# A graph network in one core: h and the attended rows turned by DMA instead of TensorE, biases side by side, a new order of work

## Time and profile before

| | |
|---|---|
| three runs | 2445.72, 2445.99, 2448.67 us; median 2445.99 |
| profiled execution | 2447.97 us, its span 2445.9 us |
| TensorE busy | 2336.1 us (96%), granted clock 0.98 in the mean |
| VectorE, ScalarE, GpSimd busy | 1980.6 (81%), 1848.4 (76%), 1636.8 us (67%) |
| DMA | 164.96 MB in 480426 packets |

### The profile page before, as it was taken

The page is one execution under the profiler, slowest core; times in us unless marked ns, Lnnn a source line. Parts: engine busy times, 40 slices in busy tenths (PEclk is TensorE's granted clock), DMA queues, the critical chain, the costliest instruction groups (busy, mean ns, idle before and its releaser), DMA issues.

```text
span 2445.9 us, 79908 instructions
## 1 busy us (share of the span) xinstructions
PE 2336.1 (96%) x26448; PEld 1722.6 (70%) x26448; DVE 1980.6 (81%) x8952; ACT 1848.4 (76%) x4660; POOL 1636.8 (67%) x2194
## 2 busy tenths in 40 slices
PE   4599999999999999999999999999999999999985
PEld 3367777777777777777777777777777777777753
DVE  7668888888888888888888888888888888888863
ACT  4467788777778877878777787877777777777763
POOL 1147677767767776777777677777767777776762
PEclk8799999999999999999999999999999999999997
DMA  6113333333323333333333333233333323333321
GB/s 201 55 37 64 60 69 65 72 66 66 68 60 67 67 70 68 67 68 60 67 68 67 70 65 70 60 67 68 67 69 65 70 60 67 67 68 69 60 50 36
DMA packets 480426, 164.96 MB, mean 67 GB/s; under 512 B 414224, under 2 KB 480016, under 8 KB 480016
## 3 DMA queue, kind: packets, MB, share of 16 engines
q1 hardware_dynamic: 479008, 159.86, 31.9%
q10 hardware_dynamic: 1008, 0.00, 0.0%
HBM read 46.53 MB, written 12.58 MB: 24 GB/s over the span
## 4 chain that ended last, share of the span: by engine, by line
PE 83%; POOL 4%; issue 3%; DMA 2%; DVE 2%; ACT 0%; SPq 0%; DVEq 0%; POOLq 0%; ACTq 0%
PE bank L146 21%; PE bank L148 21%; PE bank L147 21%; PE bank L1536 4%; PE bank L1474 4%; PE bank L1523 2%; DMA pT<-p 2%; PE bank L1430 2%; PE bank L1490 1%; PE bank L1492 1%; PE bank L1491 1%; PE bank L1581 1%; PE bank L1579 1%; PE bank L1578 1%; POOL p L629 1%
## 5 line engine op out<-in xcount | busy, mean ns | idle before, releaser
L146 PE MATMUL bank<-w_hi,dir_hT_hi 128*128 128x384 f16 x1728 | 564.5, 327 | 0.0
L148 PE MATMUL bank<-w_hi,dir_hT_lo 128*128 128x384 f16 x1728 | 564.5, 327 | 0.0
L147 PE MATMUL bank<-w_lo,dir_hT_hi 128*128 128x384 f16 x1728 | 564.4, 327 | 0.0
L765 ACT ACTIVATE probs<-minus_scores,minus_max 128x128 f32<-128x128 f32 x1536 | 488.2, 395 | 75.6 <-DVE minus_max L1017 75.6
L629 POOL TENSOR_TENSOR p<-probs,p 128x512 f16<-128x512 f32 x384 | 447.5, 1166 | 124.0 <-ACT p L772 124.0
L146 PE MATMUL bank<-hT_hi,w_hi 128*128 128x128 f16 x2304 | 400.4, 220 | 6.5 <-DVE w_lo L301 3.3
L147 PE MATMUL bank<-hT_lo,w_hi 128*128 128x128 f16 x2304 | 400.4, 220 | 0.0
L148 PE MATMUL bank<-hT_hi,w_lo 128*128 128x128 f16 x2304 | 400.3, 220 | 0.0
L1017 DVE CUSTOM_DVE_ANT_0 minus_scores<-bank,minus_score_bias 128x128 f32<-128x128 f32 x1536 | 343.2, 285 | 16.1 <-issue 13.5
L637 POOL TENSOR_TENSOR raw_weights<-raw_weights,gain_offset 128x384 f32<-128x384 f32 x192 | 192.4, 1002 | 151.5 <-ACT raw_weights L852 151.5
L147 PEld LDWEIGHTS bank<-w_lo,dir_hT_hi 128*128 128x128 f16 x1728 | 169.5, 98 | 112.7 <-issue 1.3
(11 more groups left out here) (177 smaller groups left out, 7259.4 us busy)
## 6 DMA issues: line engine op xcount, KB each, us to landing
x<-in_x SPq DMA_DIRECT2D x64, 192.0 KB, 2.5
dir_adj_tile<-in_adj SPq DMA_DIRECT2D x192, 64.0 KB, 2.1
out<-raw_weights SPq DMA_DIRECT2D x64, 192.0 KB, 2.1
adj_tile<-in_adj SPq DMA_DIRECT2D x128, 64.0 KB, 2.1
pT<-p SPq DMA_TRANSPOSE x384, 3.1
raw_weights<-in_L_gnn_Wq SPq DMA_DIRECT2D x2, 576.0 KB, 4.8
raw_weights<-in_L_gnn_Wk SPq DMA_DIRECT2D x2, 576.0 KB, 5.9
raw_weights<-in_L_gnn_Wv SPq DMA_DIRECT2D x2, 576.0 KB, 7.6
```

The lines of the kernel that those rows point to most:

```text
L146: pe.matmul(out, stat[0], move[0], start=first, stop=False)
L147: pe.matmul(out, stat[0], move[1], start=False, stop=False)
L148: return pe.matmul(out, stat[1], move[0], start=False, stop=last)
L765: last = act.activation(probs[:, i, :], scores[:, i, :], ACT.Exp, bias=nmax[:, t.slot(), i:i + 1], scale=-1.0)
```

## The change

1. h is split before it is turned: ScalarE makes the high half of h from SBUF (`att_hi`, `dir_hi`), GpSimd (`att_lo`) or VectorE (`dir_lo`) the low half, both f16, side by side (`h16`, `dh16`); one DMA transpose on SP's queue (`turn_h`, `dir_turn_h`) turns both halves at once. The attended rows of `last` likewise: scaled in place in PSUM, split (`attended_hi`, `attended_lo`), turned (`turn_o`). All f32 transposes of TensorE in the rounds but `turn_e` go.
2. `bias_rows` also holds the own bias in rows 64 and 96. The right bias is added with rows 0 to 63 and the own bias with rows 64 to 127, one right after the other (`right_self_biases`); the left bias uses rows 0 to 63.
3. A new list of steps for every engine. `project_left` of `lower` and the steps that follow on its similarity move from the end of a round to the start of the next, `project_v` of `last` one round earlier, `project_self` behind `project_right`, the write of the result two rounds later (`LAST_ROUND` is 5 instead of 3 behind). `h16`, `dh16` and x's load get more lead. The small loads of ACT's queue move to SP's.

```diff
-OPENED, LAST_ROUND = 1, G - 1 + 3
+OPENED, LAST_ROUND = 1, G - 1 + 5
...
-                low = bias_rows[32:33, first:first + 3]
...
+                for row, of in ((32, slice(0, 3)), (96, slice(1, 2))):
+                    low = bias_rows[row:row + 1, first + of.start:first + of.stop]
+                    dve.scalar_tensor_tensor(out=low, in0=self.raw_bias[row:row + 1, of],
...
+                def turn_h(t):
+                    if t is None:
+                        return
+                    wait_apart(sp, (hT_ready, t.count(-1, 16)), (h_lo, t.count()), (v_psum, t.count(-2)))
+                    sp.dma_start_transpose(hT[:, t.slot(), :, :],
+                                           h16[t.slot()][:, :, :].rearrange("p a n -> p (a n)")).then_inc(hT_ready, 16)
+
+                def turn_o(t):
...
+                def dir_turn_h(t):
+                    if t is None:
+                        return
+                    wait_apart(sp, (d["hT_ready"], t.count(-1, 16)), (d["h_lo"], t.count()), (d["u_psum"], t.count(-2)),
+                               (d["r_psum"], t.count(-2)), (d["s_psum"], t.count(-2)))
+                    sp.dma_start_transpose(dhT[:, t.slot(), :, :],
+                                           dh16[t.slot()].rearrange("p a n -> p (a n)")).then_inc(d["hT_ready"], 16)
...
                 def step(n_):
+                    att_load_adj(n_.first(-2))
+                    write(n_.last(5))
                     dir_load_adj(n_.single(0))
+                    turn_probs(n_.last(3), 0)
+                    dir_turn_h(n_.single(0))
                     turn_probs(n_.last(3), 2)
-                    load_x(n_.first(-2))
-                    turn_probs(n_.last(3), 0)
+                    turn_probs(n_.last(3), 1)
+                    turn_h(n_.last(2))
+                    dir_turn_h(n_.upper(1))
                     dir_load_adj(n_.upper(1))
-                    turn_probs(n_.last(3), 1)
+                    turn_o(n_.last(3))
                     turn_probs(n_.first(-1), 0)
-                    att_load_adj(n_.first(-2))
                     turn_probs(n_.first(-1), 1)
                     turn_probs(n_.first(-1), 2)
                     dir_load_adj(n_.lower(0))
                     att_load_adj(n_.last(1))
-                    write(n_.last(3))
+                    dir_turn_h(n_.lower(0))
+                    turn_h(n_.first(-2))
+                    load_x(n_.first(-3))
...
+                def att_lo(t):
+                    if t is None:
+                        return
+                    wait(pool, h_hi, t.count())
+                    pool.tensor_tensor(h16[t.slot()][:, 1, :], h[:, :], h16[t.slot()][:, 0, :], ALU.subtract).then_inc(h_lo, 1)
...
+                def dir_hi(t):
...
+                    act.activation(dh16[t.slot()][:, 0, :], dh[:, :], ACT.Copy).then_inc(d["h_hi"], 1)
...
+                def dir_lo(t):
+                    if t is None:
+                        return
+                    wait(dve, d["h_hi"], t.count())
+                    dve.tensor_tensor(dh16[t.slot()][:, 1, :], dh[:, :], dh16[t.slot()][:, 0, :], ALU.subtract).then_inc(d["h_lo"], 1)
...
+                def bias_of(t, part, bank, rows):
+                    pe.matmul(bank[:, 0:D], each_32nd[rows, :], bias_rows[rows, ROW[t.kind] + part, :], start=True, stop=False)
+
                 def project(t, part, bank, ready):
-                    weights, w = WEIGHTS[t.kind], part
-                    pe.matmul(bank[:, 0:D], first_and_33rd[:, :], bias_rows[:, ROW[t.kind] + part, :], start=True, stop=False)
...
+                def right_self_biases(t):
+                    if t is None:
+                        return
+                    wait(pe, d["l_lo"], t.count())
+                    wait(pe, d["ctx_ready"], t.count(-1))
+                    bias_of(t, 2, r_bank, slice(0, 64))
+                    bias_of(t, 1, own_bank, slice(64, 128))
```

More of the change, by code:

```diff
@@ L223, in __init__ @@
                 self.count["turned"] += len(self.work) if transposed else 0
-                self.count["bias"] += keeps if transposed and groups[0][1] else 0
+                self.count["bias"] += 1 if groups[0][1] else 0
                 self.count["kept"] += keeps
@@ L516, in _ @@
                 W2_upper.load_vectors(sp)
+                turn_h(first[1])
+                load_x(first[2])
+                att_load_adj(first[2])
                 dir_load_adj(single[0])
-                load_x(first[2])
+                dir_turn_h(single[0])
                 W2.ready(sp)
@@ L526, in _ @@
                 dir_load_adj(lower[0])
+                dir_turn_h(lower[0])
+                turn_h(first[2])
+                load_x(first[3])
                 run_rounds(step)
@@ new lines, in step @@
+                    left_hi(n_.lower(1))
+                    dir_input(n_.single(0))
+                    dir_hi(n_.single(0))
+                    norm_context(n_.upper(2))
+                    sides_hi(n_.lower(1))
+                    exponents(n_.last(3), 2)
+                    right_hi(n_.lower(1))
+                    v_hi_split(n_.last(3))
+                    weighted_own(n_.lower(1))
+                    probs_hi(n_.last(3), 1)
+                    probs_hi(n_.last(3), 2)
+                    q_evict(n_.first(-1))
@@ L1242, in step @@
                     scaled_denominator(n_.lower(1))
+                    v_lo_split(n_.last(3))
+                    scaled_eps(n_.lower(1))
+                    drop_masked(n_.first(-2))
+                    add_to_x(n_.upper(2))
+                    att_stats(n_.last(2))
+                    att_mean_var(n_.last(2))
+                    att_stats(n_.first(-2))
+                    att_var_eps(n_.last(2))
+                    row_max(n_.single(0))
                     context(n_.lower(1))
-                    scaled_eps(n_.lower(1))
@@ L1284, in step @@
+                    dir_lo(n_.lower(0))
                     denominator(n_.upper(1))
[L1285 to L1293 removed]
@@ L1619, in step @@
                     combine(n_.upper(1))
+                    project_v(n_.last(2))
                     similarity(n_.lower(0))
-                    project_left(n_.lower(0))
-                    att_turn_h(n_.first(-2))
-                    project_self(n_.lower(0))
                 def turn_v_bias(pe):
@@ L1687, in _ @@
                 similarity(lower[0])
-                project_left(lower[0])
-                att_turn_h(first[2])
-                project_self(lower[0])
                 run_rounds(step)
```

534 lines of the change are left out of this document (243 added, 291 removed).

## The result

The changed kernel takes 2482.24 us in the median of four runs (2480.00 to 2482.86), the kernel before 2446.25 beside it (2445.72 to 2448.67): ratio 1.0143, 95% interval 1.0126 to 1.0161. It is 36 us slower where I forecast 46 faster.

What follows compares the result with a forecast made beforehand. TensorE was taken to bound the kernel, busy 35.64 of each 35.70 us round. Transposes -127, bias pair -31, row-split visits +88, late operands +13, prologue and tail +10 sum to -47: 2400 us, range 2330 to 2460.

Steps and rivals of the forecast that it cites:

- rival B: Turned h of `single` comes late each round and shifts TensorE's work behind `similarity`: slower, 2510 or 2475 us; chance 0.20.
- Transposes -127: TensorE's 1152 transposes of h and `attended` go, 0.11 us each, all on the path: -127 us.
- pair -31: Right and own bias run side by side on 64 rows each, saving one 0.162 us slot 192 times: -31 us.
- A visit to 64 rows at 0.23: Each bias visit to another row split on TensorE costs 0.23 us, 384 times: +88 us (0 to +119).
- rival A: Change of row split on TensorE is nearly free with f16 weights: 2325 us, or 2360 at 0.1 per visit; chance 0.25.
- Landing 3.1 us: SP's new transposes of 768 columns land 3.1 us after issue, bounds 3.0 and 5.3, or 2.3 by columns.
- I take 0.2 us a round of late operands: +13: In the rounds the new order mostly hides the longer turns; TensorE waits 0.2 us a round: +13 us (0 to +50).
- rival C: Time saved comes back as waits at several places (p's transposes on SP, combine of upper): 2430 to 2451 us; chance 0.10.
- `drop_masked` goes earlier ... nothing: Moving `drop_masked` earlier, with statistics waiting on the engine's own earlier work, costs nothing.
- hidden by the splitting of W0: Small loads moved to SP's queue behind `turn_h(first[0])` delay W1's vectors some 5 us, hidden by W0's splitting.
- Tail +8 for three turns: The last graph's chain crosses three new turns (upper, last, attended), 2.6 us longer each: 8 us.
- Own behind right costs nothing in the rounds: Self part following the right part in every project costs nothing in the rounds, 1.6 us per layer in the tail.

Runs made afterwards that it cites:

- the run on the kernel before: Kernel before, with its nine bias matmuls a round over rows 0 to 63 instead of all 128: 2555.05 us.
- the swap: Kernel after, with VectorE's low half of upper's rows (`dir_lo`) put ahead of single's context: 2460.95 us.
- the best version: Kernel after with masks and one turn reordered at the start, upper's low half ahead of single's context, biases over all 128 rows: 2420.00 us, ratio 0.9888 to before.
- the last run: Kernel after with many list moves and all-row biases (2425.04), plus earlier split of first's second probabilities chunk, K's eviction and last's first maxima: 2499.68 us, ratio 1.0211.

## Why the prediction was wrong

The forecast was 2400 in 2330 to 2460. The result is above the range, in the band that I gave rival B (2475 to 2510, chance 0.20), but not by B's mechanism alone, as shown below.

- **Transposes -127, pair -31: right.** Together 158 / 64 = 2.47 us a round of pitches; measured 2.4 to 2.5.
- **A visit to 64 rows at 0.23: right, a little high.** 0.19 and 0.21 at the places shown, 0.19 in the run on the kernel before; rival A is out. By the Trainium skill's TensorEngine Tiling (Array Packing), key properties, a change of tiling mode drains the engine: the trace agrees in so far as it has a pause on either side, 0.09 us going in and 0.10 coming out. The Trainium skill's price for a pair, in TensorE: Matmul & The Clock Gate, packing small matmuls (one matmul and about 4 ns), holds between the two of the pair, 3 ns apart here, and not for the pair among full matmuls, where it takes 0.26 and another 0.11 ahead of it.
- **Landing 3.1 us, DMA share up to 0.58, GpSimd at 27.6: near enough.** 2.7 to 2.8 in the median, 0.50 to 0.59, 27.1 to 28.5.
- **"I take 0.2 us a round of late operands: +13": the step that failed.** It was 1.4 a round, some +90, beyond my upper end of 50. Rival B has the kind of mechanism, at the wrong place. I worked out one chain step by step, `first` to `single`, and called it the tightest; its turned rows land 1.6 us ahead of use. Of `upper` I wrote that its 22 us hold chains of "16 to 19 us, with more room", from a count of steps ("about twice as many"). Between the similarities of `lower` and `upper` lie 23.2 us in the kernel after, and `upper`'s turned rows land 0.14 to 0.3 us ahead of use: with its standing in the engines' lists the chain takes 23, not 16 to 19. The swap shows what this place costs: 21 us for half a us. I had added latency at six hand-overs a graph and worked out one.
- **What B and C had right.** Waits on turned h were to be some 10 us, over 60 for B; turned direction and attended rows have 22.8 in the 55 rounds. The rest of the 62 is K, p and the own result, at several places as rival C had it. That the time lies in B's band is the sum of these and of the prologue, and in part chance. Nor does the swap account for the 90: the best version still has 53 us of such waits, so most of them are shown to be late operands, but not by which chain.
- **"`drop_masked` goes earlier ... nothing" and "hidden by the splitting of W0", prologue +1.7: failed too.** It cost 22.9 us, 20 of them by these steps. I costed a step moved to the front of a list at nothing and didn't ask when its operand lands (14.1 us). The loads moved on SyncE I followed, the turn behind W1's wait and its loads I did not. All of it was in the diff.
- **Tail +8 for three turns:** 1.7. What covered the rest stays open.
- **Own behind right costs nothing in the rounds:** not tested by itself. With ScalarE's new list the old order costs 143 us more.

Put together with what was measured: -151 for the pitches, +69 for changes of rows (1.1 a round, net of those of the kernel before), +90 waits, +23 prologue, +2 tail: +33, for a measured +36. The packing of the biases alone is a loss: three edits that keep the DMA turns and drop the row split make the change a gain of 27 us.

What stays open: why rounds are uneven (35.2 beside 38). I took late landings for turns that meet turns; the traces say otherwise. Of the 165 turns of direction rows in the 55 rounds, 29 take over 3.0 us to land. An earlier turn was under way at 11 of these 29, and at 67 of the other 136. But at all 29 a packet of the kind that the page calls `instruction` (0.9 us in the median) ran within the 2.7 us after the issue, and of the 87 turns without one none was late; without the loads' bytes it was 32 of 83, and none of 82. One such turn, issued at 1346.05, with its stretch of the DMA view:

```profile
q8 instruction: 1, 0.02, 2.1%
...
dir_hT<-raw_weights SPq DMA_TRANSPOSE x1, 4.4
```

At `upper` such turns have 12.9 of the 18.2 us that TensorE waits there. That is found side by side, not tried by a run, and the length of a round was not traced to it. Nor was the chain that sets the 35.09 us of the best version found; both large waits of its list are candidates, and the last run shows that this list alone doesn't tell.

## What to carry to other kernels

When an edit makes a hand-over 2.6 us longer at six places, price all six against the work that the engine has between their ends, and find where the producer's half stands in the list of its own engine. The largest line in a view of waits need not be the one that sets the time: K's, with 19.0 us, went to 0.6 in a run that was 29 us slower. Swap or delay one operand and look at what moves. And a step put first in a list costs until its operand is there; a transfer put behind large loads lands behind them, too.

## What the runs showed of the hardware

- A DMA turn of 128 x 768 fp16 takes 2.7 us from issue to landing in the median and holds SyncE's queue for 1.21; one of a 128 x 128 table holds it for 1.12, so its size hardly counts there. The landing view of the kernel after, of `dir_hT` and then of `pT` (1024 columns):

```profile
DMA to landing us min/median/max: 2.7/2.7/7.5
...
DMA to landing us min/median/max: 3.0/3.3/5.9
```

- The same turn took 9.4 us to land when it was issued behind eight loads (three of 576 KB, five of 192 KB) and 2.8 ahead of them.
- In the rounds of the kernel after, turns of direction rows take over 3.0 us to land only where an `instruction` packet ran beside them: 29 of 78, against none of 87.
- A matmul over 64 of 128 rows between full ones costs 0.19 to 0.21 us more, with f16 weights too, not only before f32 scores. Two such, over different halves, start 3 ns apart.
